# A new order of all jobs in a fused attention and expert kernel, with two more low halves of W1 made by TensorE and ScalarE

## The reference

```python
xn = layernorm(x)
# attention, causal, over each of the 2 sequences
scores = einsum('bsd,de,bte->bst', xn, qk, xn) / sqrt(128)
attn   = softmax(where(causal, scores, -inf))
a      = einsum('bst,btd,de->bse', attn, xn, ov)
# expert network: each of the 4096 rows goes to one expert of 8
aff    = xn @ centroids.T
eid    = argmax(aff);  alpha = sigmoid(aff[eid])
xln    = layernorm(xn) * ln_g[eid] + ln_b[eid]
ffn    = relu(xln @ w1[eid] + b1[eid]) @ w2[eid] + b2[eid]     # 128 -> 512 -> 128
out    = x + a + (xn + alpha * ffn)
```

## Time and profile before

| | before |
|---|---|
| time, median of 3 | 231.22 us (231.13 to 231.58) |
| the profiled execution's own time | 231.44 us |
| its span | 229.7 us, so 1.74 us lie outside the span |
| TensorE busy | 213.2 us, 93% of the span |
| VectorE busy | 178.7 us, 78% |
| ScalarE busy | 150.5 us, 66% |
| GpSimd busy | 153.6 us, 67% |
| mean granted clock of TensorE | 0.977 |

### The profile page before, as it was taken

How to read it: one execution, slowest core, us unless ns; L and a number is a source line. 1 busy time by engine, 2 the same in 40 slices (tenths; PEclk the granted TensorE clock), 3 DMA queues, 4 the chain that set the end, 5 groups by cost and what they waited for, 6 DMA issues and landing times.

```text
span 229.7 us, 6818 instructions
## 1 busy us (share of the span) xinstructions
PE 213.2 (93%) x2418; PEld 165.0 (72%) x2418; DVE 178.7 (78%) x441; ACT 150.5 (66%) x333; POOL 153.6 (67%) x224
## 2 busy tenths in 40 slices
...
GB/s 178 279 300 56 49 125 252 189 119 3 1 45 38 35 49 36 39 36 48 37 38 36 144 135 129 126 144 127 101 131 143 36 41 44 37 32 184 211 200 148
DMA packets 41345, 23.55 MB, mean 103 GB/s; under 512 B 12472, under 2 KB 39136, under 8 KB 41312
## 3 DMA queue, kind: packets, MB, share of 16 engines
...
q10 hardware_dynamic: 336, 0.14, 0.2%
...
## 4 chain that ended last, share of the span: by engine, by line
PE 68%; DVE 19%; issue 6%; DMA 3%; SPq 2%; ACT 1%; DVEq 0%; ACTq 0%
PE psum L1324 6%; PE psum L1292 6%; PE psum L1290 5%; PE psum L1291 5%; PE psum L1267 5%; PE psum L1422 4%; PE psum L1341 4%; PE psum L1424 4%; PE psum L1423 4%; PE psum L1333 4%; PE psum L1334 4%; PE psum L1450 4%; PE psum L1449 4%; PE psum L1448 4%; DVE xn L791 3%
## 5 line engine op out<-in xcount | busy, mean ns | idle before, releaser
L1042 ACT ACTIVATE p_sb<-psum 128x512 f32<-128x512 f32 (+1 forms) x80 | 41.9, 536 | 15.1 <-PE psum L1324 7.5
L685 POOL DMA_INDIRECT sorted_y<-xn x39 | 38.8, 996 | 17.4 <-ACT xn L1165 11.0
L902 DVE TENSOR_TENSOR p_lo<-p_sb,p_hi 128x512 f16<-128x512 f32 (+3 forms) x56 | 36.7, 678 | 13.8 <-ACT p_sb L1042 13.7
L1010 DVE SCALAR_TENSOR_TENSOR h_lo<-psum,h_hi 128x512 f16<-128x512 f32 x39 | 26.8, 690 | 22.3 <-ACT h_hi L1157 22.1
L663 POOL MEMSET idle<- 1x600 f32 x71 | 41.7, 588 | 0.0
L1036 ACT ACTIVATE p_hi<-psum 128x512 f16<-128x512 f32 (+3 forms) x56 | 30.2, 543 | 17.6 <-PE psum L1341 9.8
L676 POOL DMA_INDIRECT sorted_x<-xr,pos x32 | 32.5, 1014 | 8.6 <-issue 8.4
L1157 ACT ACTIVATE h_hi<-psum 128x512 f16<-128x512 f32 x39 | 23.2, 597 | 22.1 <-PE psum L1424 20.4
L887 DVE TENSOR_REDUCE row_max<-psum 128x1 f32<-128x512 f32 x48 | 31.3, 682 | 3.4 <-PE psum L1267 3.1
L1267 PE MATMUL psum<-kT_hi,qT_hi 128*128 128x512 f16 (+3 forms) x80 | 25.1, 360 | 7.3 <-DVE row_max L887 5.5
L1422 PE MATMUL psum<-v_full,w_hl 128*128 128x128 f16 x156 | 29.0, 224 | 0.3 <-issue 0.2
...
## 6 DMA issues: line engine op xcount, KB each, us to landing
...
sorted_y<-xn POOLq DMA_INDIRECT x39
...
```

The costliest lines, as they stand in the source:

```text
L685: pool.indirect_dma_start(out=sorted_y[:, :], out_offset=bass.IndirectOffsetOnAxis(ap=tokens, axis=0), in_=xs[:, t % SLOTS, 0:P], in_offse ...
L1042: a.activation(p_sb[:, u, off:GW], bank[SCORE[n % R]][:, off:GW], ACT.Exp, scale=SCALE).then_inc(s_exp, 1)
```

## The change

`LOW_BY_TENSOR` goes from 4 to 6, so experts 4 and 5 get their low halves of W1 from TensorE and ScalarE. `ORDER` is replaced as a whole; only a piece of it is shown, since the rows below say what it does. No function is changed.

```diff
-M.0.1.3.1 MR.0.1.3.1 M.0.1.2.1 MR.0.1.2.1 M.0.1.0.1 MR.0.1.0.1 M.0.1.1.1 MR.0.1.1.1 ROW.4.8 W1.4 M.0.1.0.0 MR.0.1.0.0
+MR.0.2.1.1 X.1 ROW.4.8 SH.0.1 X.2 M.0.2.3.2 MR.0.2.3.2 P.0 P.1 P.2 M.0.2.0.0 MR.0.2.0.0 M.0.2.2.0 MR.0.2.2.0 X.3 X.4
...
-    LOW_BY_TENSOR = 4
+    LOW_BY_TENSOR = 6
```

More of the change, by code:

```diff
@@ L68 @@
 ORDER = entries("""
[L69 to L73, removed]
@@ L79 @@
[L79 to L83, removed]
@@ L84 @@
[L84 to L98, removed]
@@ L124 @@
[L124 to L127, removed]
+MISC LE.0.1 VAR.0.1 VAR.1.2 WU C0 C1 C2 BIASa T.0 W1.0 T.1 W1.1 W1b.0 W1b.1 V.0 V.1 Q.0 Q.1 RN.0.1 RN.1.2 RN.2.3
@@ new lines @@
+BASE.0 BASE.1 RN.3.4 LE.1.2 C1a C0a AE.0 C2a Ta.0 AE.1 AE.2 Ta.1 W1h.0 W1h.1 AE.3 AE.4 LE.2.3 W1l.0 W1l.1 LE.3.4 Vf.0
+Qa.0 Vf.1 XA.2 AE.5 Qa.1 ROW.0.1 BIAS C2v C1v ROW.1.2 VAR.2.3 Tl.0 Tl.1 VAR.3.4 VAR.4.8 Ql.0 Ql.1 W1.2 T.2 W2l.0
+RN.4.8 W2l.1 BASE.2 BASE.3 W2l.2 W1.3 BASE.4 BASE.5 BASE.6 COL0 BASE.7 Tl.2 M.0.0.0.0 MR.0.0.0.0 M.0.0.3.0 MR.0.0.3.0
+M.0.0.1.0 MR.0.0.1.0 M.0.0.2.0 MR.0.0.2.0 RM.0.0 M.0.1.3.1 MR.0.1.3.1 M.0.1.3.0 MR.0.1.3.0 M.0.1.2.1 MR.0.1.2.1 W1b.2
+W1b.3 M.0.1.0.0 MR.0.1.0.0 M.0.1.1.0 MR.0.1.1.0 M.0.1.2.0 MR.0.1.2.0 R2 W1.4 SH.0.0 M.0.1.0.1 MR.0.1.0.1 Ta.2 W1h.2
@@ new lines @@
+W1h.3 W2.0 W2.1 LE.4.8 W1l.2 W1l.3 XA.3 SHa.0.0 Qa.2 W1h.4 W1h.5 W2.2 W1l.4 W1l.5 EX.0 EX.1 EX.2 SHa.0.1 R2a XA.5 XA.7
+EX.3 EX.4 W2.3 EX.5 Ta.3 Ta.4 Ta.5 Ta.6 Ta.7 EX.6 Qa.3 Sh.0 Va.0 Va.1 Sh.1 Sh.2 Sh.3 Sh.4 Sh.5 EX.7 EX.8 EX.9 EX.10
+W2.4 Q.2 W1.5 M.0.1.1.1 Ql.2 X.0 MR.0.1.1.1 M.0.2.2.1 RM.0.1 MR.0.2.2.1 W1b.4 W1b.5 M.0.2.3.1 MR.0.2.3.1 M.0.2.1.1
+MR.0.2.1.1 X.1 ROW.4.8 SH.0.1 X.2 M.0.2.3.2 MR.0.2.3.2 P.0 P.1 P.2 M.0.2.0.0 MR.0.2.0.0 M.0.2.2.0 MR.0.2.2.0 X.3 X.4
+M.0.2.0.2 MR.0.2.0.2 M.0.2.3.0 MR.0.2.3.0 M.0.2.1.2 MR.0.2.1.2 M.0.2.1.0 MR.0.2.1.0 M.0.2.2.2 MR.0.2.2.2 M.0.2.0.1
```

77 lines of the change are left out of this document (48 added, 29 removed).

## The result

| | before | changed |
|---|---|---|
| time, median of 9 | 231.91 us (231.13 to 232.29) | 230.54 us (229.11 to 230.88) |
| ratio | | 0.9934, 95% interval 0.9909 to 0.9958 |
| profiled execution, its span | 231.44, 229.7 | 230.55, 228.8 |
| first send | 67.82 | 64.79 |
| first expert product | 131.25 | 130.05 |

The ratio is that of the mean times, without executions over 1.5% longer than the fastest of their kernel. The forecast was 227.3 us with a range from 224.6 to 230.3. The changed kernel is faster, but by 1.4 to 1.5 us, not by 4, and its median lies just outside the range. The kernel before itself measured 0.7 us longer in these nine executions (231.91) than in the three that the forecast started from (231.22), so the gain says more than the median: it is a third of the forecast's. The front came earlier about as was said; most of it was lost again in one place near 125 us.

What follows compares the result with a forecast made beforehand. VectorE was taken to bound the front, TensorE the rest. Held time -4.3, low halves -1.2 and +0.5, early order +0.9 sum to -4.1 us: 231.44 to 227.3, range 224.6 to 230.3.

Steps and rivals of the forecast that it cites:

- The normalisation: Eight normalisations in VectorE's front, set apart from GpSimd's large operations: 3.4 us in place of 8.07, held 1.2 not 5.9.
- `R2`: Two small VectorE products now among GpSimd's operations: held 1.0 us, one operation, with bounds 0 and 4.6.
- the rival with 4.6: VectorE held in its new places too: `R2` held 4.6 us, rest as forecast, gives 230.9; slower than before, chance 0.08.
- The small instructions: `neg_max` and the correction step on VectorE, held 1.3 us before beside GpSimd: 0.7 held after, bounds 0 and 1.3.
- The early order: Around the third group's input at 11.04 us, VectorE's work moves behind the transfer: costs 0.9 us, bounds 0 and 1.2.
- The low halves of W1: Two low halves leave VectorE in the front, saving 1.2 us; TensorE pays 0.5 for two matmuls.
- The front into the sends: The sends start behind positions VectorE computes, so move with the front: first send at 63 to 65 us, before 67.82.
- The step that failed: At the sends' end, GpSimd's last three low halves of W2 meet a `p_lo` as before: change 0.
- a burst that misses: GpSimd's three operations at the sends' end miss `p_lo`: 2.5 us better than the forecast, 224.8; chance 0.14.
- The rival of the late sends: Sends don't move with the front because `Vl.2` waits for late values: 230 to 231.2 us; chance 0.11, shared with longer holds.
- The forecast's own case: Whole kernel, each term within its bounds: 226.0 to 229.0 us, chance 0.62.
- ScalarE's price: ScalarE's 2 x 0.58 us for the two low halves of W1, taken as hidden in idle time; otherwise 1.2 at most.

Runs made afterwards that it cites:

- the run with the burst later: Changed kernel, but GpSimd waits ahead of expert 5's low half of W2 until VectorE has made `p_lo` of step 51: 224.90 us, ratio 0.9716.

## Why the prediction was wrong

**The normalisation.** Forecast 3.4 us, measured 2.98, with one of the eight held. Right.

**`R2`.** Forecast 1.0 held, measured 1.07 (1.44 less 0.37), by one of GpSimd's operations. Right; the rival with 4.6 did not come.

**The small instructions.** Forecast 0.7 held. Measured 0.8, over three of them (0.45 at 45.39, the rest at 39.03 and 22.84). Right.

**The early order.** Forecast 0.9. The third group's statistics wait 0.67 us, and the first queries' low half comes at 19.12, 0.8 later. Right as a delay; putting `kT_lo` back returned 0.3.

**The low halves of W1.** Forecast a net 0.7. The second of the two rows it was read from, at 34.82, is a maximum (line 887) and not a low half; that one stands at 35.80. The pitch is 0.6 us there too, so the 1.2 stands. Undone, the time rises by 1.6 us (0.5 to 2.6), so the term may be too small, but 0.7 isn't excluded.

**The front into the sends.** Forecast a first send at 63 to 65 us; it was 64.79. TensorE's first softmax scores came 5.5 us earlier (28.5, against 34.0), but VectorE had 2.93 us of idle time before 55.97, waiting for TensorE, whose clock was at 0.51 from 50.0 to 53.4 while it was busy all 3.40 us:

```profile
50.00:53.40 3.40, 3.40 (x22) 3.34 (x21) 2.77 (x10) 0.24 (x1) 0.00 (x0) 0.51 0.30 81
```

```profile
55.97 0.69 DVE L887 TENSOR_REDUCE row_max<-psum 128x1 f32<-128x512 f32 x1 [2.93 <-PE psum L1267]
```

In the run with the burst later, in which it did not fall there, the first send was at 63.51. I had counted no clock: the lower stretches of the earlier trace rows went, and others came.

**The step that failed** is "At their end, `W2l.5` to `W2l.7` stand as before and meet a `p_lo`; ... I take 0 for both." The order of GpSimd was the same, but that of VectorE was new, and the sends and VectorE's work moved by different amounts. The three operations held one `p_lo` in either kernel, for 4.20 and 4.52 us, but in the changed one at a point where TensorE had little else to do: it was busy 1.73 of 4.20 us, before 3.08 of 4.30. The meeting costs 5.1 us in the changed kernel and 1.8 before, by taking it away in each. That is 3.3 us, and forecast plus this term is 230.6, against 230.54 measured. That they agree to 0.1 us is luck, since the term is uncertain by 1.4; that it is about what is missing isn't. I had named its opposite, a burst that misses, with a chance of 0.14, and wrote that a shift of 0.3 us decides; but as a rival that only gains. The case in which it costs more belonged beside it, with 2.5 us of idle time and a stretch at the lower clock as its price.

**The rivals and the range.** The rival of the late sends had 230 to 231.2 us, and the measured time lies there, but by another way: the sends did move with the front (64.79), and the product followed by only 1.2 us. The forecast's own case was called each term within its bounds, 226.0 to 229.0. With all terms at one end the sum gives 223.5, at the other 232.9 (and 1.2 more if ScalarE's price shows), so that stretch was narrower than its bounds, and the 0.62 on it too high for them.

**The rule of the Trainium skill** ("SBUF — State Buffer", section "Who interferes with whom": whoever issues first has the shared ports for one whole instruction) fits the normalisations and `R2`, one operation each, and the instructions with one large operand in PSUM, which ran free. It does not fit `p_lo`: 4.20 and 4.52 us through three operations back to back, though both had begun ahead of the first of these, by 0.28 and 0.60 us. There the measurement decides.
